# Reading the first two blocks' rows ahead of the second block's weights, in a two-layer cross-attention and experts kernel

## The chip, the cores and the metric

The kernel runs on one core of one Trainium2 chip. The metric is device time of one execution in microseconds (us): the median of three timed runs. Lower is better. One further execution was recorded by the hardware profiler. All rows below come from that one.

## The reference

The input is 8 x 512 tokens of width 256. Two layers follow each other. Each adds gated cross-attention and a gated feed-forward part. Only the last part matters here, the second layer's feed-forward, a mixture of 8 experts with the best 2 for each token:

```python
logits = x @ gate_w + gate_b                       # x: layernormed tokens, [4096, 256]
probs = softmax(logits); top_w, top_idx = top_k(probs, 2)
top_w = top_w / sum(top_w)
h = silu(x @ w1[e]) * (x @ w3[e])                  # for each expert e; w1, w3: 256 x 1024
out_e = h @ w2[e]                                  # w2: 1024 x 256
x = x + tanh(g_ffn[1]) * sum over the token's two experts of top_w * out_e
```

## The kernel before

The kernel is three stages, each in a program block of its own: `first_layer`, `cross_attention` and `experts`. A program block ends only when all engines have reached its end, and the engines then start the next one together.

Cross-attention also does the routing. For each token it finds two experts, and GpSimd (POOL) writes the token's row (256 values, its weight and its number) with an indirect DMA to two places of a table in HBM, `xs` (`expert_in` in the trace), one region for each expert. This is the scatter; each of its DMAs adds 16 to `routing.scattered` when it lands.

`experts` has two program blocks. The first, "route", does what remains once the last tokens are routed:

- POOL issues the last 8 scatter DMAs (L766) and waits for `routing.scattered` to reach its full count (L1711).
- VectorE (DVE) works out on one partition which expert and which first row each of the NBLK = 39 blocks of 256 rows has (L1727 to L1748). The results are the tiles `first_row` and `expert`. It then signals `blocks_known`.
- SyncE (SP) issues the weights of block 0 and of block 1 (`load_weights`). Each is three DMAs of 1 MB into the three tiles `raw[0..2]` (`m_raw`). There is one set of raw tiles, so block 1's load of `raw[n]` waits on `lo_done[n]`, until block 0's copy has been split out of it.
- ScalarE (ACT) rounds each raw tile to `w_hi` (`high_part`, L1673) and DVE takes the remainder to `w_lo` (`low_part`, L1677), for block 0 only.
- SP ends this program block by waiting until block 1's three weight tiles have landed (L1702).

The second, "run", is the experts' part: 39 blocks with two sets of tiles (`p` = 0 and 1). TensorE (PE) transposes the block's rows (`turn`, L1845), ACT and DVE split them, PE multiplies by w1 and w3 in three passes (`hidden`, 96 matmuls), and by w2 (`project`, 48 matmuls, L1852). While block j is computed, ACT and DVE split the weights of block j + 1: ACT's `high_part(j + 1)` of the tile n stands in its order behind the silu of f = 1, 3 and 5 of block j. SP in this block loads rows (`load`, L1787 and L1789) and then weights for each block j > 1, in a written order. POOL gathers the rows of the output that a block adds to (`fetch`, L1812) and scatters them back (`store`, L1819).

The order at the start of "run" before the change: SP loads the rows of blocks 0 and 1, then goes on with block 2's rows and weights. PE's first instruction is `turn(0, 0, 0)`, which waits on `x_in[0]`, that is, on the rows of block 0. A load of rows needs two things: a register load of the first row's number from `first_row`, and that the scatter has landed.

Of the kernel before, what the change touches and what calls it, by code (L numbers as in the profile page):

```python
# [11 lines left out]
P = 128  # L12
BATCH, SEQ, D = 8, 512, 256
T = BATCH * SEQ
NT = T // P
# [5 lines left out]
NE, TOPK = 8, 2  # L21
BLK = 256
NBLK = T * TOPK // BLK + NE - 1
ROWS = NE * T + NE * BLK
BT = BLK // P
WIDE = D + 2
# [737 lines left out]
def scatter_rows(pool, routing, xs, k, j):  # L764

    pool.indirect_dma_start(out=xs, out_offset=bass.IndirectOffsetOnAxis(ap=routing.pos[:, k, j:j + 1], axis=0),  # L766
                            in_=routing.XN[:, j, :], in_offset=None).then_inc(routing.scattered, 16)
# [863 lines left out]
def experts(nc, M1, X, ident_f, routing, xs, out):  # L1631
# [10 lines left out]
    with ExitStack() as ctx:  # L1642
        sb = lambda n, s, d=F32: ctx.enter_context(nc.sbuf_tensor("m_" + n, s, d))
        sem = lambda n: ctx.enter_context(nc.semaphore("m_" + n))
        two = lambda n, s, d=F32: [sb(f"{n}{p}", s, d) for p in range(2)]
        pair = lambda n: [sem(n + "0"), sem(n + "1")]
        expert = sb("expert", [1, NBLK], I32)
        first_row = sb("first_row", [1, NBLK], I32)
# [7 lines left out]
        w_raw_in = [sem(f"w_raw_in{n}") for n in range(3)]  # L1656
        hi_done, lo_done = [sem(f"hi_done{n}") for n in range(3)], [sem(f"lo_done{n}") for n in range(3)]
        h_ps, y_ps = sem("h_ps"), sem("y_ps")

        def load_weights(sp, j):  # L1660

            e = sp.value_load(expert[0:1, j:j + 1] if isinstance(j, int) else expert[0:1, bass.ds(j, 1)],
                              min_val=0, max_val=NE - 1)
            for n, w in enumerate((w1, w3, w2)):
                if not (isinstance(j, int) and j == 0):
                    sp.wait_ge(lo_done[n], j)
                sp.dma_start(raw[n][:, :, :], w[e].rearrange("(c p) n -> p c n", p=P)).then_inc(w_raw_in[n], 16)

        def high_part(act, j, p, n):
            act.wait_ge(w_raw_in[n], 16 * (j + 1))  # L1670
            if not (isinstance(j, int) and j < 2):
                act.wait_ge(*((h_ps, FC * (j - 1)) if n < 2 else (y_ps, BT * (j - 1))))
            act.activation(w_hi[p][n][:, :, :], raw[n][:, :, :], ACT.Copy).then_inc(hi_done[n], 1)  # L1673
# [8 lines left out]
        with ExitStack() as route:  # L1682
            sb = lambda n, s, d=F32: route.enter_context(nc.sbuf_tensor("r_" + n, s, d))
            sem_ = lambda n: route.enter_context(nc.semaphore("r_" + n))
            starts_i, starts = sb("starts_i", [1, NBLK, NE], I32), sb("starts", [1, NBLK, NE])
            per_e = lambda n, d=F32: sb(n, [1, NE], d)
            total, total_i, padded_i, padded, ends = per_e("total"), per_e("total_i", I32), per_e("padded_i", I32), per_e("padded"), per_e("ends")
            off = [per_e("off0"), per_e("off1")]
            past, skipped = sb("past", [1, NBLK, NE]), sb("skipped", [1, NBLK, NE])
            per_b = lambda n: sb(n, [1, NBLK])  # L1690
            n_past, sum_past, at, number = per_b("n_past"), per_b("sum_past"), per_b("at"), per_b("number")
            iotas, chain, blocks_known = sem_("iotas"), sem_("chain"), sem_("blocks_known")
            block = route.enter_context(nc.Block())
            B = BATCH - 1

            @block.sync
            def _(sp):
                sp.wait_ge(blocks_known, 1)
                load_weights(sp, 0)
                load_weights(sp, 1)  # L1700
                for n in range(3):
                    sp.wait_ge(w_raw_in[n], 32)  # L1702

            @block.gpsimd
            def _(pool):
                pool.iota(starts_i[:, :, :], pattern=[[BLK, NBLK], [0, NE]], base=0, channel_multiplier=0).then_inc(iotas, 1)
                for k in range(TOPK):
                    pool.wait_ge(routing.labelled, TOPK * B + k + 1)
                    for j in range(TPB):
                        scatter_rows(pool, routing, xs, k, j)  # L1710
                pool.wait_ge(routing.scattered, 16 * NT * TOPK)  # L1711

            @block.scalar
            def _(act):
                for n in range(3):
                    high_part(act, 0, 0, n)

            @block.vector
            def _(dve):
                steps = Steps(dve, chain)  # L1720

                def do(ins):

                    steps.done(ins)
                    steps.wait()

                do(dve.tensor_tensor(total[:, :], routing.ends_at[0:1, :], routing.region[0:1, :], ALU.subtract))  # L1727
                do(dve.tensor_scalar_add(total_i[:, :], total[:, :], float(BLK - 1)))
                do(dve.tensor_scalar(padded_i[:, :], total_i[:, :], -BLK, None, ALU.bitwise_and))
                do(dve.tensor_copy(padded[:, :], padded_i[:, :]))  # L1730
                do(dve.memset(off[0][:, 0:1], 0.0))
                do(dve.tensor_copy(off[0][:, 1:NE], padded[:, 0:NE - 1]))
                c, s = 0, 1
                while s < NE:
                    do(dve.tensor_copy(off[1 - c][:, 0:s], off[c][:, 0:s]))
                    do(dve.tensor_tensor(off[1 - c][:, s:NE], off[c][:, s:NE], off[c][:, 0:NE - s], ALU.add))
                    c, s = 1 - c, 2 * s
                do(dve.tensor_tensor(ends[:, :], off[c][:, :], padded[:, :], ALU.add))
                dve.wait_ge(iotas, 1)
                do(dve.tensor_copy(starts[:, :, :], starts_i[:, :, :]))  # L1740
                do(dve.tensor_tensor(past[:, :, :], starts[:, :, :], ends[:, :].unsqueeze(1).broadcast_to([1, NBLK, NE]), ALU.is_ge))
                do(dve.tensor_reduce(n_past[:, :], past[:, :, :], AX.X, ALU.add))
                do(dve.tensor_tensor(skipped[:, :, :], past[:, :, :], padded[:, :].unsqueeze(1).broadcast_to([1, NBLK, NE]), ALU.mult))
                do(dve.tensor_reduce(sum_past[:, :], skipped[:, :, :], AX.X, ALU.add))
                do(dve.scalar_tensor_tensor(out=at[:, :], in0=n_past[:, :], scalar=float(T), in1=starts[:, :, 0], op0=ALU.mult, op1=ALU.add))
                do(dve.tensor_tensor(number[:, :], at[:, :], sum_past[:, :], ALU.subtract))
                do(dve.tensor_copy(first_row[:, :], number[:, :]))
                dve.tensor_scalar(expert[:, :], n_past[:, :], float(NE - 1), None, ALU.min).then_inc(blocks_known, 1)  # L1748
                relabel(dve, routing, B)
                for n in range(3):  # L1750
                    low_part(dve, 0, 0, n)

        with ExitStack() as run:
            sb = lambda n, s, d=F32: run.enter_context(nc.sbuf_tensor("e_" + n, s, d))
            sem_ = lambda n: run.enter_context(nc.semaphore("e_" + n))
            two = lambda n, s, d=F32: [sb(f"{n}{p}", s, d) for p in range(2)]
            pair = lambda n: [sem_(n + "0"), sem_(n + "1")]
            w_hi[1] = [sb(f"hi1_{n}", shapes[n], F32R) for n in range(3)]
            w_lo[1] = [sb(f"lo1_{n}", shapes[n], F32R) for n in range(3)]
            xb = two("x", [P, BT, WIDE])  # L1760
            label = two("label", [P, BT, 2])
            x_hi, x_lo = two("x_hi", [P, KC, BLK], F32R), two("x_lo", [P, KC, BLK], F32R)
            silu = [X[:, n, :] for n in range(2)]
# [4 lines left out]
            ps_h = [ps[:, 2 + n, :] for n in range(4)]  # L1768
            ps_y = [ps[:, 6 + n, 0:D] for n in range(2)]

            x_in, x_used = pair("x_in"), pair("x_used")
            x_hi_done, x_lo_done = sem_("x_hi_done"), sem_("x_lo_done")
            silu_done, gated_done, g_parts = sem_("silu_done"), sem_("gated_done"), sem_("g_parts")
            g_high, y_left, y_out = sem_("g_high"), sem_("y_left"), sem_("y_out")
            labelled, blanks, before_in = sem_("labelled"), sem_("blanks"), sem_("before_in")
# [5 lines left out]
            @block.sync  # L1781
            def _(sp):
                def load(j, i, p):
                    if not (isinstance(j, int) and j < 2):
                        sp.wait_ge(x_used[p], i)
                        sp.wait_ge(labelled, j - 1)
                    at = sp.value_load(first_row[0:1, j:j + 1] if isinstance(j, int) else first_row[0:1, bass.ds(j, 1)],  # L1787
                                       min_val=0, max_val=ROWS - BLK)
                    sp.dma_start(xb[p][:, :, :], xs[bass.ds(at, BLK), :].rearrange("(n p) d -> p n d", p=P)).then_inc(x_in[p], 16)  # L1789
                    if not (isinstance(j, int) and j < 2):  # L1790
                        load_weights(sp, j)

                load(0, 0, 0)
                load(1, 0, 1)
                with sp.Fori(1, LAST // 2) as i:
                    for p in range(2):
                        load(2 * i + p, i, p)
                load(LAST, LAST // 2, 0)
# [275 lines left out]
```

## Time and profile before

| | |
|---|---|
| median of 3 runs | 2155.09 us (2154.49 to 2155.93) |
| profiled execution | 2156.33 us |
| its span | 2154.6 us |
| mean granted TensorE clock | 0.944 |
| PE busy | 1913.3 us (89%) |
| DVE busy | 1601.9 us (74%) |
| ACT busy | 1069.0 us (50%) |
| POOL busy | 919.2 us (43%) |

The span runs from the first to the last recorded instruction. The profiled execution's own time is 1.73 us longer than its span. Busy shares are means over three stages with different limits, so what a change in one place is worth has to be read from that place: from the waits and the chain of work there. An engine named with a q (SPq) is that engine's sequencer, which also issues DMAs.

### The profile page before, as it was taken

Reading aid. Unit: us, or ns where it says so; the run is one execution under the profiler, and the core shown is the slowest. Engines: PE = TensorE matmul, PEld = TensorE weight load, DVE = VectorE, ACT = ScalarE, POOL = GpSimd, SP = SyncE. Lnnn points to the kernel's source line nnn. Section 1 sums busy time; section 2 is a strip of 40 time slices with the busy share of each in tenths; the row PEclk is TensorE's granted clock in tenths of the full one; section 3 lists DMA queues with packets and bytes.
Section 4 is the critical chain, followed back from the end, with each engine's and each line's share of the span. In section 5 each row is a group of like instructions: output and inputs, shape, how many; then the busy total and the mean of one; then the engine's idle time right before and its main releaser. Section 6 shows DMA issues by size and latency. Waiting matters only on the chain. (4 is left out here: it accounts for less than half of the span.)

```text
span 2154.6 us, 35704 instructions
## 1 busy us (share of the span) xinstructions
PE 1913.3 (89%) x11904; PEld 1347.0 (63%) x11968; DVE 1601.9 (74%) x3393; ACT 1069.0 (50%) x2062; POOL 919.2 (43%) x682
## 2 busy tenths in 40 slices
PE   5889898987669999999999999919999999999998
PEld 2566666665323343343434343419999999999998
DVE  7999999997546667767776778436777777777775
ACT  2233334433326655555555555415656555556663
POOL 6988888884533334343534331111222222222222
PEclk8899999998859999999999999958999999999999
DMA  5222222220243251515142441045766666666661
GB/s 169 109 89 87 109 86 89 87 94 1 61 100 87 63 123 45 128 45 123 65 110 93 89 121 33 21 146 171 227 225 214 219 225 219 219 228 227 224 209 59
DMA packets 140065, 271.45 MB, mean 126 GB/s; under 512 B 13915, under 2 KB 91823, under 8 KB 134066
## 3 DMA queue, kind: packets, MB, share of 16 engines
q1 hardware_dynamic: 128812, 244.55, 36.7%
q0 software_dynamic: 10624, 25.26, 3.2%
q8 instruction: 56, 0.92, 0.2%
q14 instruction: 55, 0.45, 0.1%
q10 hardware_dynamic: 518, 0.27, 0.0%
HBM read 201.96 MB, written 71.39 MB: 127 GB/s over the span
## 5 line engine op out<-in xcount | busy, mean ns | idle before, releaser
L1434 DVE CUSTOM_DVE_ANT_0 x_dump<-x_ps,x_bias_q 128x512 bf16<-128x512 f32 x512 | 353.2, 690 | 100.6 <-PE x_ps L1127 87.9
L1303 ACT ACTIVATE x_PT<-x_ps 128x512 f32<-128x512 f32 x512 | 292.2, 601 | 225.7 <-PE x_ps L1142 222.6
L1819 POOL DMA_INDIRECT out_dram<-e_y,e_label x78 | 78.9, 1011 | 369.4 <-DVE e_y L1971 357.5
L1915 ACT ACTIVATE X<-m_ps 128x256 f32<-128x256 f32 x312 | 119.1, 382 | 232.6 <-PE m_ps L1852 232.6
L1127 PE MATMUL x_ps<-x_KS,x_QS 96*128 96x512 bf16 x512 | 201.3, 395 | 23.3 <-DVE x_mx L1434 22.6
L1142 PE MATMUL x_ps<-x_QS,x_KS 98*128 98x512 bf16 x512 | 195.7, 382 | 6.7 <-issue 2.6
L1954 DVE TENSOR_TENSOR X<-X,m_ps 128x256 f32<-128x256 f32 x312 | 120.9, 418 | 103.5 <-ACT X L1915 98.9
L1852 PE MATMUL m_ps<-e_x_lo,m_hi 128*128 128x256 f32 x640 | 181.4, 283 | 1.5 <-DVE e_x_lo L1939 1.5
L1852 PE MATMUL m_ps<-e_x_hi,m_lo 128*128 128x256 f32 x640 | 181.3, 283 | 0.0
L1852 PE MATMUL m_ps<-e_x_hi,m_hi 128*128 128x256 f32 x640 | 181.1, 283 | 0.0
L1141 PE MATMUL x_ps<-x_bias_k,x_ident_b 128*128 128x512 bf16 x448 | 171.3, 382 | 1.1 <-issue 1.1
L1852 PE MATMUL m_ps<-e_x_hi,e_hi 128*128 128x256 f32 x608 | 171.1, 281 | 0.0
L1852 PE MATMUL m_ps<-e_x_hi,e_lo 128*128 128x256 f32 x608 | 171.1, 281 | 0.0
L1852 PE MATMUL m_ps<-e_x_lo,e_hi 128*128 128x256 f32 x608 | 171.1, 281 | 0.0
L1677 DVE TENSOR_TENSOR m_lo<-m_raw,m_hi 128x2048 fp32r<-128x2048 f32 x60 | 137.3, 2289 | 36.4 <-ACT m_hi L1673 36.4
L285 POOL TENSOR_TENSOR a_pool_pv<-a_e,a_v 128x2304 f32<-128x2304 f32 x32 | 162.2, 5070 | 0.0
L1812 POOL DMA_INDIRECT e_y<-out_dram,e_label x78 | 82.8, 1061 | 163.7 <-DMA out_dram<-e_y,e_label 136.7
L1677 DVE TENSOR_TENSOR e_lo<-m_raw,e_hi 128x2048 fp32r<-128x2048 f32 x57 | 130.4, 2287 | 26.2 <-ACT e_hi L1673 26.2
L1127 PEld LDWEIGHTS x_ps<-x_KS,x_QS 96*128 96x128 bf16 x512 | 49.9, 98 | 141.7 <-DVE x_mx L1434 110.3
L1673 ACT ACTIVATE m_hi<-m_raw 128x2048 fp32r<-128x2048 f32 x60 | 115.0, 1917 | 20.8 <-DMA m_raw<-in_L_ffn_w_dram 20.8
L1852 PEld LDWEIGHTS m_ps<-e_x_lo,m_hi 128*128 128x128 f32 x640 | 121.7, 190 | 1.9 <-issue 1.9
L1852 PEld LDWEIGHTS m_ps<-e_x_hi,m_lo 128*128 128x128 f32 x640 | 121.7, 190 | 0.0
(301 smaller groups left out, 5409.1 us busy)
## 6 DMA issues: line engine op xcount, KB each, us to landing
m_raw<-in_L_ffn_w_dram SPq DMA_DIRECT2D x117, 1024.0 KB, 5.3
expert_in<-a_blank SPq DMA_DIRECT2D x34, 1032.0 KB, 4.3
parts<-x_part SPq DMA_DIRECT2D x24, 512.0 KB, 3.7
e_x<-expert_in SPq DMA_DIRECT2D x39, 258.0 KB, 4.8
next_mask_k<-in_maskT_dram SPq DMA_DIRECT2D x32, 256.0 KB, 2.6
next_mask_q<-in_mask_dram SPq DMA_DIRECT2D x29, 256.0 KB, 2.8
x_KS<-parts SPq DMA_DIRECT2D x16, 384.0 KB, 11.4
x_QS<-parts SPq DMA_DIRECT2D x8, 576.0 KB, 6.6
```

The lines of the kernel that those rows point to most:

```text
L285: pool.tensor_tensor(heads(pool_pv[:, :], PV_POOL), probabilities(e_[t % 2][:, PV_OWN * H:], PV_POOL), values(v_sb[t % 3][:, :], PV_POOL), ...
L1127: pe.matmul(ps_max[m % 2], QS[b % 2][0:HROWS, h, q * P:(q + 1) * P], KS[b % 2][0:HROWS, h, :], start=True, stop=True).then_inc(s1_ps, 1)
L1141: pe.matmul(ps_st[e % 3], ident_b[:, :], bias_k[b % 2][:, kc, :], start=True, stop=False)
L1142: pe.matmul(ps_st[e % 3], KS[b % 2][:, h, kc * P:(kc + 1) * P], QS[b % 2][0:HROWS + MROWS, h, :], start=False, stop=True).then_inc(st_read ...
L1303: act.activation(PT[unit % 2][:, k, :], ps_st[e % 3], ACT.Exp, scale=DH ** -0.5).then_inc(exp_done, 1)
L1434: dve.tensor_tensor_reduce(out=dump[:, :], in0=ps_max[m % 2], in1=bias_q[b % 2][:, q, :], scale=1.0, scalar=NEG, op0=ALU.add, op1=ALU.max, ...
L1673: act.activation(w_hi[p][n][:, :, :], raw[n][:, :, :], ACT.Copy).then_inc(hi_done[n], 1)
L1677: eng.tensor_tensor(w_lo[p][n][:, :, :], raw[n][:, :, :], w_hi[p][n][:, :, :].bitcast(F32), ALU.subtract)\
L1812: pool.indirect_dma_start(out=yb[p][:, n, :], out_offset=None, in_=rows, in_offset=tokens(p, n), bounds_check=T - 1, oob_is_err=False).the ...
L1852: mm = pe.matmul(out, left[a], right[b], start=first and n == 0, stop=last and n == 2)
L1915: act.activation(silu[f % 2], ps_h[f % 4][:, 0:BLK], ACT.Silu).then_inc(silu_done, 1)
L1954: dve.tensor_tensor(gated[k % 2][:, n, :], silu[n], ps_h[f % 4][:, BLK:2 * BLK], ALU.mult)\
```

## The change

In "route", SP no longer loads block 1's weights and no longer waits for them. It issues block 0's weights, waits until the whole scatter has landed, and then issues the rows of blocks 0 and 1. The row tiles `xb` and their semaphores `x_in` are allocated earlier so that this is possible. In "run", SP begins with block 1's weights. It then goes on with the loads of block 2 as before. The loads of blocks 2 to 38 keep their waits and their order.

```diff
+        xb = two("x", [P, BT, WIDE])
+        x_in = pair("x_in")
+
+        def load_rows(sp, j, p):
+            at = sp.value_load(first_row[0:1, j:j + 1] if isinstance(j, int) else first_row[0:1, bass.ds(j, 1)],
+                               min_val=0, max_val=ROWS - BLK)
+            sp.dma_start(xb[p][:, :, :], xs[bass.ds(at, BLK), :].rearrange("(n p) d -> p n d", p=P)).then_inc(x_in[p], 16)
...
                 sp.wait_ge(blocks_known, 1)
                 load_weights(sp, 0)
-                load_weights(sp, 1)
-                for n in range(3):
-                    sp.wait_ge(w_raw_in[n], 32)
+                sp.wait_ge(routing.scattered, 16 * NT * TOPK)
+                for j in range(2):
+                    load_rows(sp, j, j)
...
                 def load(j, i, p):
-                    if not (isinstance(j, int) and j < 2):
-                        sp.wait_ge(x_used[p], i)
-                        sp.wait_ge(labelled, j - 1)
-                    at = sp.value_load(...)
-                    sp.dma_start(xb[p][:, :, :], ...).then_inc(x_in[p], 16)
-                    if not (isinstance(j, int) and j < 2):
-                        load_weights(sp, j)
-
-                load(0, 0, 0)
-                load(1, 0, 1)
+                    sp.wait_ge(x_used[p], i)
+                    sp.wait_ge(labelled, j - 1)
+                    load_rows(sp, j, p)
+                    load_weights(sp, j)
+
+                load_weights(sp, 1)
                 with sp.Fori(1, LAST // 2) as i:
```

## Rows read from the trace of the kernel before

**Rows 1.** Chain of work that ended last, 1380 to 1462: start us, us, what.
```profile
1453.66 0.27 SPq L1787
...
1454.41 2.80 DMA e_x<-expert_in
...
1457.25 1.13 PE m_ps L1845 x4
```

**Rows 2.** The same chain, whole span, its longest pieces.
```profile
1459.87 14.14 PE m_ps L1852 x96
1474.45 17.14 PE m_ps L1852 x144
...
2122.87 22.79 PE m_ps L1852 x192
```

**Rows 3.** Waits of the SP queue, 1427 to 1454: us in total, times, longest.
```profile
SPq L1702 <- DMA m_raw<-in_L_ffn_w_dram: 7.7, 1, 7.7
```

**Rows 4.** Timeline of SP: start us, us, engine line op, count.
```profile
1427.55 1.45 SPq L1667 DMA_DIRECT2D m_raw<-in_L_ffn_w_dram  x3
...
1437.15 0.39 SPq L1667 DMA_DIRECT2D m_raw<-in_L_ffn_w_dram  x1
...
1445.15 0.37 SPq L1667 DMA_DIRECT2D m_raw<-in_L_ffn_w_dram  x1
...
1454.41 1.54 SPq L1789 DMA_DIRECT2D e_x<-expert_in  x2
```

**Rows 5.** Line L1667, 1427 to 1430, then 1437 to 1446: issue to landing.
```profile
DMA to landing us min/median/max: 5.2/9.2/12.3
...
DMA to landing us min/median/max: 6.2/6.7/8.0
```

**Rows 6.** Timeline 1415 to 1460, all engines; brackets hold idle before, and releaser.
```profile
1419.84 0.16 DVE L1620 COPY ends_at<-x_prior 128x8 f32<-128x8 f32 x1
...
1420.31 0.15 DVE L1727 TENSOR_TENSOR r_total<-ends_at,region 1x8 f32<-1x8 f32 x1 [0.30 <-PEq L780]
...
1432.16 0.96 POOL L766 DMA_INDIRECT expert_in<-XN,pos  x1 [0.30 <-issue]
...
1437.29 1.91 ACT L1673 ACTIVATE m_hi<-m_raw 128x2048 fp32r<-128x2048 f32 x1 [2.64 <-DMA m_raw<-in_L_ffn_w_dram]
1439.23 2.29 DVE L1677 TENSOR_TENSOR m_lo<-m_raw,m_hi 128x2048 fp32r<-128x2048 f32 x1 [2.26 <-ACT m_hi L1673]
1440.89 1.91 ACT L1673 ACTIVATE m_hi<-m_raw 128x2048 fp32r<-128x2048 f32 x1 [1.70 <-DMA m_raw<-in_L_ffn_w_dram]
...
1442.84 2.29 DVE L1677 TENSOR_TENSOR m_lo<-m_raw,m_hi 128x2048 fp32r<-128x2048 f32 x1 [1.31 <-ACT m_hi L1673]
1453.67 0.99 POOL L1823 MEMSET e_y<- 128x512 f32 x2 [20.55 <-POOLq L1682]
```

**Rows 7.** DMA queues, 1437.5 to 1438, then 1450 to 1453: packets, MB, share.
```profile
q0 software_dynamic: 2, 0.00, 0.2%
...
q1 hardware_dynamic: 74, 0.07, 7.0%
```

**Rows 8.** Timelines of ACT and DVE in block 0 of "run".
```profile
1465.65 1.91 ACT L1673 ACTIVATE e_hi<-m_raw 128x2048 fp32r<-128x2048 f32 x1
...
1468.63 1.91 ACT L1673 ACTIVATE e_hi<-m_raw 128x2048 fp32r<-128x2048 f32 x1
...
1471.48 1.93 ACT L1673 ACTIVATE e_hi<-m_raw 128x2048 fp32r<-128x2048 f32 x1
...
1475.44 1.48 DVE L1964 TENSOR_TENSOR e_g_lo<-X,e_g_hi 128x512 fp32r<-128x512 f32 x2
```

**Rows 9.** Windows: us; busy PE, PEld, DVE, ACT, POOL; PEclk, DMA share, GB/s.
```profile
1465.00:1466.00 1.00, 1.00 (x8) 1.00 (x8) 0.21 (x1) 0.63 (x2) 0.00 (x0) 0.74 0.00 0
...
556.00:558.00 2.00, 2.00 (x4) 0.35 (x2) 0.19 (x1) 0.00 (x0) 2.00 (x13) 0.61 1.00 292
```

**Rows 10.** Timeline of PE, start of the cross-attention stage.
```profile
554.67 3.39 PE L1093 MATMUL x_ps<-next_wkv,next_cT 128*128 128x512 f32 x4 [2.46 <-POOL x_half L977]
```

**Rows 11.** The page, DMA queues, whole span: packets, MB, share of 16 engines.
```profile
q8 instruction: 56, 0.92, 0.2%
```

More of the change, by code:

```diff
@@ L1759, in experts @@
             w_lo[1] = [sb(f"lo1_{n}", shapes[n], F32R) for n in range(3)]
-            xb = two("x", [P, BT, WIDE])
             label = two("label", [P, BT, 2])
@@ L1769, in experts @@
             ps_y = [ps[:, 6 + n, 0:D] for n in range(2)]
-            x_in, x_used = pair("x_in"), pair("x_used")
+            x_used = pair("x_used")
             x_hi_done, x_lo_done = sem_("x_hi_done"), sem_("x_lo_done")
@@ L1783, in load @@
                 def load(j, i, p):
-                    if not (isinstance(j, int) and j < 2):
-                        sp.wait_ge(x_used[p], i)
-                        sp.wait_ge(labelled, j - 1)
-                    at = sp.value_load(first_row[0:1, j:j + 1] if isinstance(j, int) else first_row[0:1, bass.ds(j, 1)],
-                                       min_val=0, max_val=ROWS - BLK)
-                    sp.dma_start(xb[p][:, :, :], xs[bass.ds(at, BLK), :].rearrange("(n p) d -> p n d", p=P)).then_inc(x_in[p], 16)
-                    if not (isinstance(j, int) and j < 2):
-                        load_weights(sp, j)
-                load(0, 0, 0)
-                load(1, 0, 1)
+                    sp.wait_ge(x_used[p], i)
[3 more added lines that the diff above has]
+                load_weights(sp, 1)
                 with sp.Fori(1, LAST // 2) as i:
```

## The prediction, made before the changed kernel was run

> **What bounds the kernel now.** I read the slices of the page first: PE is busy nine tenths or more in almost every slice of the experts' part, and one slice in the middle falls to one tenth. The views that matter are the ones of that hole. The chain of waits, from its end backwards, shows what the time after the hole is: one unbroken run of PE matmuls, 144 to a block, each next piece beginning where the last one ends, up to the last block [rows 2]. So whatever moves PE's first matmul of the experts' part moves the end by the same amount, unless a new gap opens later.
>
> Ahead of that run the chain holds SP's register load, the DMA of block 0's rows (2.80 us), and the four transposes at 1457.25 [rows 1]. SP starts this only at 1453.66, because every engine starts "run" together. What is late then? The waits of the SP queue name it: 7.7 us at L1702, on block 1's weights [rows 3]. The last of them was issued at 1445.15 [rows 4] and took 8.0 us to land [rows 5], so it landed at 1453.15. The other engines were done before: POOL had issued its last scatter by 1433.12 and then stood idle until 1453.67, and DVE's last split of block 0's weights ended at 1442.84 + 2.29 = 1445.13 [rows 6]. PE needs none of block 1's weights to start. It waits for a barrier that waits for them, and then for rows whose table has long been complete.
>
> **The change, part by part.**
>
> *Wait at L1702 removed.* The end of "route" becomes the latest of the other arrivals. DVE's is 1445.13.
>
> *Does SP arrive later than DVE?* It now waits for the scatter. The last packets of the scatter's queue (q0) are in the half microsecond to 1438 [rows 7]. The semaphore comes after the last packet, by an amount that no row gives alone; I allow 0 to 1 us, so 1438 to 1439. A register load and the issue behind it took 1454.41 - 1453.66 = 0.75 us, and the second rows' DMA ended its issue 1.54 us after the first began [rows 1, 4]. SP therefore issues block 0's rows at 1438.8 to 1439.8 and is through at 1440.3 to 1441.3, at least 3.8 us before DVE. Cost nothing, covered by DVE's and ACT's splits; without that cover it would be up to 2 us.
>
> *Do the rows land in time?* They lie behind block 0's third weight tile, which lands at 1440.9 (ACT takes it at 1440.89 [rows 6]). Their own time is 2.8 us [rows 1]. So block 0's rows land between 1442.6 and 1443.7, ahead of 1445.13. The row DMA's 2.8 us leaves the path.
>
> *Does block 0's third weight tile land earlier?* Block 1's first tile was issued at 1437.15 [rows 4], while it was still under way; now 0.5 MB of rows follow later instead of that 1 MB. From below the gain is nothing. From above it is what DVE allows: its second split ends at 1439.23 + 2.29 = 1441.52, so the third cannot start before 1441.5 instead of 1442.84, 1.3 us. The tail of block 1's last load speaks for nothing: from 1450 to 1453 the engines were 7.0% busy [rows 7], about one of 16, so a single engine finished alone at its own pace, with nobody to compete with. I take 0.
>
> *Barrier and PE's start.* From DVE's end to its next instruction across the previous barrier: 1419.84 + 0.16 to 1420.31, 0.31 us. Across this one: 1453.15 to 1453.66, 0.5 us [rows 1, 6]. I take 0.45 us, so PE's transposes start at 1445.6 instead of 1457.25.
>
> **Sum: 1457.25 - 1445.6 = 11.65 us less.** What follows the transposes (ACT, its table load, DVE, first matmul at 1459.87) keeps its lengths.
>
> *Block 1's weights moved into "run".* Three DMAs and one register load stand ahead of block 2's on SP. All three `lo_done` waits are already met. Their issue begins about 0.75 us after the barrier, at 1446.35, the others about 0.5 us apart each (three in 1.45 us [rows 4]). When they land I take from block 0's own load, also three at once with indirect traffic beside it: 5.2, 9.2 and 12.3 us after issue [rows 5], hence 1451.6, 1456.1 and 1459.7. When they are needed: ACT took them at 1465.65, 1468.63 and 1471.48 [rows 8], 8.40, 11.38 and 14.23 us after the transposes began, hence now 1454.0, 1457.0 and 1459.8. Each is just in time, the third by 0.1 us. There is more cover behind that: `project` starts at 1474.45, its third quarter (12 matmuls of 17.14/144 = 0.119 us each, 1.43 us a quarter) at 1477.3, and the third remainder it needs ended at about 1475.44 + 0.7 = 1476.1 [rows 2, 8]. So ACT may be 1.2 us late before PE waits. Cost 0; if that cover is gone, each microsecond of lateness beyond it is one microsecond of time.
>
> The page "DMA: Bandwidth & Descriptors" of the Trainium skill (section "Anatomy of one DMA") fits a DMA of the GpSimd path by about 2.0 us plus its bytes over 436 GB/s. For 3 x 1.05 MB issued together that would be 9.2 us, against 13.3 us from first issue to last landing in block 0's load here; by it the third tile would come at about 1455.6, over 4 us early, and the case of late weights below would fall away. The trace doesn't agree, and I go by the trace.
>
> *What is queued behind them on SP:* block 2's rows. Their wait on `labelled` is met at about 1448, after the weights' issue at 1447.8; nothing is held up. They lie behind 3 MB in the queue, landing by about 1461, and PE turns block 2 only after 1474.45 + 17.14 = 1491.6 [rows 2], less 11.65, 1480. Block 2's weights wait for DVE's splits as before. POOL's first `fetch` waits on DVE's label, not on SP, and its sum is wanted after `project`, over 20 us later. The steady state then has the same instructions, waits and bytes as before.
>
> *The clock.* In the profile the granted clock rose from half (1.2 GHz) to full (2.4 GHz) inside 1465 to 1466, mean 0.74 [rows 9], so at about 1465.5, some 5.6 us after the first matmul. At the start of cross-attention it rose inside 556 to 558 (mean 0.61, so about 1.56 us in), 2.9 us after PE began at 554.67 [rows 9, 10]. Half speed costs half its time. A rise 2.7 us sooner or later gives or takes 1.3 us. I take the same 5.6 us and keep 1.3 for the range.
>
> The profiled execution would take 2156.33 - 11.65 = 2144.7 us, and the median, 1.24 us below it, 2155.09 - 11.65 = **2143.4 us**.
>
> **The rivals.**
>
> *A. The third tile lands early as well* (up to 1.3 us more). Against it the lone engine of [rows 7]; for it the traffic taken away at 1437. 2142.1 us, chance 0.05.
>
> *B. Block 1's weights come late and PE waits for ACT.* For it: the margins of 0.1 to 2.4 us above, a register load slower than 0.75 us, and POOL's first gather beside them. Against it: block 0's load had the scatter beside it, which is no less. Third tile 2.5 to 5 us later than counted: PE waits 1.2 to 3.7 us, 2144.6 to 2147.1, centre 2145.8 us. Chance 0.10.
>
> *C. The change doesn't do what it says:* SP's scatter wait or the rows take the place of the weights' landing at 1453. It decides from 1445.13 on; no time is saved only if the rows land 10 us later than counted. The last q0 packets before 1438 speak against it. The same page of the skill says that the semaphore follows the last byte's receipt, slowest where the target is HBM, and puts most of its 2 us there; the scatter writes HBM. By that the rows would be issued by 1440.8 and land near 1443.6, still in time. 2155.1 us, chance 0.02.
>
> *D. Slower: instruction loading.* The engines' instructions come by DMA as well (56 packets, 0.92 MB on one of the queues [rows 11]). Before, "run" began with the DMA engines idle after 1453; now its code is fetched while 3 MB of weights fill them. A fetch of a PE, ACT or DVE piece that waits behind them in each of the first blocks would stop PE. It decides from 11.65 us in total; by the longest landing in this stretch, 12.3 us for each of two fetches, 24.6 - 11.65 = 13 us slower, 2168 us. Against it: block 0's splits ran at full pace while 3 MB landed, and steady blocks carry 3 MB each without a break in PE. Chance 0.03.
>
> **How the numbers follow.** My forecast has 0.80, with its own range of 2142.0 to 2144.8 (clock 1.3 us either way, barrier 0.15 us, spread of the runs 0.7 us); A 0.05, B 0.10, C 0.02, D 0.03. The range reaches down to A with a sooner clock, 2141.5, and up to the greater part of B, 2146.5. A measurement of this kernel tells a change of about 0.2% (4.3 us) from none. Forecast, A and B all lie beyond that: faster 0.95, same 0.02, slower 0.03.
>
> **What would show it right or wrong.** After: no wait at L1702; PE's first transposes about 0.45 us behind DVE's third split in "route"; two row DMAs issued near 1439 and three weight DMAs from about 1446.3; ACT's three splits of block 1's weights 8.4, 11.4 and 14.2 us behind the transposes, released by ACT's own order and not by a DMA; an unbroken chain of L1852 from then on. The forecast is wrong if ACT's third split names the weights' DMA as releaser with over 1.2 us of idle time, if SP is the last at the barrier, or if gaps open in PE in blocks 1 or 2.

## The result, and the profile after

Timed side by side, 12 runs each, the changed kernel took 2140.84 us (median, 2132.74 to 2147.83) and the kernel before 2154.55 us (2148.17 to 2160.16). The ratio is 0.9939, 95% interval 0.9923 to 0.9955: 13 us less, between 10 and 17. The forecast was 11.65 us less (0.9946) and 2143.4 us, with a range down to 2141.5; the measured time lies 0.7 us below that range. About 0.5 of these 0.7 us lie in the kernel before, which was counted from 2155.09 us in the forecast and has 2154.55 here; 0.9939 of 2155.09 would be 2141.9, inside the range. The sign and the mechanism at the hole were as forecast. Two other things happened to which the forecast's sum gave nothing: the matmuls of the odd blocks run faster, and the clock rises sooner.

The chain of waits of the kernel after, from 1440 on (start us, us, what), and its last large piece; it answers to [rows 1, 2]:

```profile
1450.91 1.10 PE m_ps L1846 x4
...
1452.04 0.61 ACT e_x_hi L1903
...
1453.51 13.39 PE m_ps L1853 x96
1466.89 0.44 PE m_ps L1846 x4
1467.33 16.99 PE m_ps L1853 x144
...
2109.84 22.57 PE m_ps L1853 x192
```

SP's register load and the DMA of the rows are gone from the chain. It goes back from the transposes straight to the barrier. But the transposes start at 1450.91, not at 1445.6 (the next paragraphs say why); and the segments of PE behind them are shorter than those in [rows 2]: 13.39 us instead of 14.14, and 16.99 instead of 17.14.

The waits of the SP queue (us in total, times, longest) answer to [rows 3]:

```profile
SPq L1663 <- DMA expert_in<-XN,pos: 9.9, 1, 9.9
...
SPq L1689 <- PEq L1689: 3.7, 1, 3.7
```

SP waits 9.9 us for the scatter, issues the rows, and then still waits 3.7 us at the barrier. It isn't the last to arrive.

The timelines (start us, us, engine line op) answer to [rows 4, 6, 8]:

```profile
1426.06 0.15 DVE L1734 TENSOR_TENSOR r_total<-ends_at,region 1x8 f32<-1x8 f32 x1 [0.30 <-PEq L780]
...
1433.32 1.45 SPq L1674 DMA_DIRECT2D m_raw<-in_L_ffn_w_dram  x3
1445.42 1.53 SPq L1665 DMA_DIRECT2D m_x<-expert_in  x2
1451.59 1.40 SPq L1674 DMA_DIRECT2D m_raw<-in_L_ffn_w_dram  x3
...
1446.36 1.91 ACT L1680 ACTIVATE m_hi<-m_raw 128x2048 fp32r<-128x2048 f32 x1 [1.07 <-DMA m_raw<-in_L_ffn_w_dram]
1448.30 2.29 DVE L1684 TENSOR_TENSOR m_lo<-m_raw,m_hi 128x2048 fp32r<-128x2048 f32 x1 [0.69 <-ACT m_hi L1680]
...
1458.67 1.91 ACT L1680 ACTIVATE e_hi<-m_raw 128x2048 fp32r<-128x2048 f32 x1
...
1461.52 1.93 ACT L1680 ACTIVATE e_hi<-m_raw 128x2048 fp32r<-128x2048 f32 x1
...
1464.40 1.93 ACT L1680 ACTIVATE e_hi<-m_raw 128x2048 fp32r<-128x2048 f32 x1
```

The first of these rows is the one to read first. Route starts at 1426.06 in this execution and at 1420.31 in that of before [rows 6]. All stages ahead of it run the same instructions in both kernels. So times after it have to be counted from it. From there to the transposes are 1450.91 - 1426.06 = 24.85 us, against 1457.25 - 1420.31 = 36.94. ACT's three splits of block 1's weights carry no bracket: no DMA held them.

For the comparisons below the span is cut into four stretches: up to the start of route (DVE's first instruction there), the *hole* (from there to PE's transposes), block 0 (from the transposes to the first segment of 144 matmuls), and the blocks (from there to PE's last matmul). In the profile before they are 1420.31, 36.94, 17.20 and 671.21 us; after, 1426.06, 24.85, 16.42 and 665.08 us.

The costliest groups (out<-in, shapes, count | busy, mean ns of one | idle before) say where the 6.1 us in the blocks come from. Of the kernel after:

```profile
L1853 PE MATMUL m_ps<-e_x_hi,m_lo 128*128 128x256 f32 x640 | 180.8, 282 | 0.0
...
L1853 PE MATMUL m_ps<-e_x_hi,e_hi 128*128 128x256 f32 x608 | 169.7, 279 | 0.0
...
L1853 PE MATMUL m_ps<-e_lo,e_g_hi 128*128 128x256 f32 x304 | 85.6, 282 | 0.0
```

Of the kernel before:

```profile
L1852 PE MATMUL m_ps<-e_x_hi,m_lo 128*128 128x256 f32 x640 | 181.3, 283 | 0.0
...
L1852 PE MATMUL m_ps<-e_x_hi,e_hi 128*128 128x256 f32 x608 | 171.1, 281 | 0.0
...
L1852 PE MATMUL m_ps<-e_lo,e_g_hi 128*128 128x256 f32 x304 | 87.1, 286 | 0.0
```

The names with m_ are the weight tiles of even blocks, those with e_ of odd blocks. Only the matmuls that read e_hi and e_lo are clearly faster, by 1 to 2 ns in `hidden` and by 4 to 5 in `project`; the means of the others changed by at most 1 ns. Nothing in the new order of loads singles out odd blocks. But the change also allocates xb (2 x 2064 bytes per partition, with rounding 4160) ahead of these six tiles instead of behind them, so they moved by 4160 bytes per partition; no other tile that L1853 reads did.

### The profile page after: what moved, and what is told of

Same layout as the page of the kernel before. It is cut to its first block and busy times, and to the rows that moved or that the text cites. A ratio compares the mean times of both kernels' runs of the same rounds, so it can differ in the third digit from the quotient of the medians.

```text
span 2141.3 us, 35766 instructions
## 1 busy us (share of the span) xinstructions
PE 1915.6 (89%) x11968; PEld 1347.2 (63%) x11968; DVE 1601.4 (75%) x3393; ACT 1068.8 (50%) x2062; POOL 923.3 (43%) x682
## 5 line engine op out<-in xcount | busy, mean ns | idle before, releaser
L1141 PE MATMUL x_ps<-x_bias_k,x_ident_b 128*128 128x512 bf16 x512 | 197.9, 386 | 2.3 <-DMA x_QS<-x_rows 1.2
L1853 PE MATMUL m_ps<-e_x_lo,m_hi 128*128 128x256 f32 x640 | 181.1, 283 | 1.5 <-DVE e_x_lo L1940 1.5
L1853 PE MATMUL m_ps<-e_x_hi,m_hi 128*128 128x256 f32 x640 | 180.9, 283 | 0.0
L1853 PE MATMUL m_ps<-e_x_hi,m_lo 128*128 128x256 f32 x640 | 180.8, 282 | 0.0
L1853 PE MATMUL m_ps<-e_x_lo,e_hi 128*128 128x256 f32 x608 | 170.3, 280 | 0.0
L1853 PE MATMUL m_ps<-e_x_hi,e_hi 128*128 128x256 f32 x608 | 169.7, 279 | 0.0
L1853 PE MATMUL m_ps<-e_x_hi,e_lo 128*128 128x256 f32 x608 | 169.6, 279 | 0.0
L1853 PEld LDWEIGHTS m_ps<-e_x_lo,m_hi 128*128 128x128 f32 x640 | 121.3, 190 | 1.9 <-issue 1.9
L1853 PEld LDWEIGHTS m_ps<-e_x_hi,m_hi 128*128 128x128 f32 x640 | 121.3, 190 | 0.0
```

What stands on the lines that cost most here:

```text
L1141: pe.matmul(ps_st[e % 3], ident_b[:, :], bias_k[b % 2][:, kc, :], start=True, stop=False)
L1853: mm = pe.matmul(out, left[a], right[b], start=first and n == 0, stop=last and n == 2)
```

## The experiments

Ratios are to the kernel before, run on the same chip. A mean over the profiles is used where single ones differ. ctl_before, g2_pad4160 and g3_xb_last were executed once each, so they give stretches and no ratio.

**ctl_before.** The kernel before, unchanged.

> The kernel before, unchanged, profiled once more. It tells what differs between executions of one program. Theory N (the differences outside the hole are spread between executions): route begins some us earlier or later than 1420.3, as it did after the change (1426.1), and the matmul segments of the experts' part differ from 17.09 us. Theory P (the pace of the experts' matmuls belongs to the place of the weight tiles): 144 matmuls take 17.08 to 17.09 us in every steady segment again, whatever the start of route.

Measured: 2156.42 us in the profiled execution. Route starts at 1422.87, the hole is 34.61 us, block 0 17.13, the blocks 671.15. So the hole of one and the same program differs by 2.3 us between two executions, while the 671 us of the blocks repeat to 0.06. The pace of the matmuls belongs to the program. The length of the hole is spread by microseconds in the old order.

**e1_place.** Only the allocation of the change, in the order of before.

```diff
+        xb = two("x", [P, BT, WIDE])
+        x_in = pair("x_in")
 
         def load_weights(sp, j):
...
-            xb = two("x", [P, BT, WIDE])
...
-            x_in, x_used = pair("x_in"), pair("x_used")
+            x_used = pair("x_used")
```

> The kernel before with only the allocation of the change: xb and x_in are allocated before the block-1 weight tiles e_hi and e_lo, which so lie 4160 bytes further on. The order of all instructions is that of before. Theory P: the matmuls that read e_hi and e_lo go from 281 ns to 279 (hidden) and 276 (project), a pair of blocks takes 34.7 us instead of 35.05, and the time falls by 6 us (0.28%), the hole staying as it was. Theory O (the pace follows from the new order of loads): pace and time as before.

Measured: 0.9969 (0.9953 to 0.9985), about 6.7 us less. Hole 35.31 us, block 0 17.48, the blocks 665.16 us. Its chain shows the two segments that were 17.14 and 17.09 us in the kernel before; from then on 17.00 and 16.85 us take turns, as after the change:

```profile
1476.30 17.06 PE m_ps L1853 x144
...
1493.80 16.86 PE m_ps L1853 x144
```

Theory P holds. Where xb is allocated is worth about half of what the change brought by the times (6.7 of 13 us) and a third by the profiles (6.1 of 17).

**e2_order.** The change, with every tile at its old address.

```diff
+        sb_e = lambda n, s, d=F32: ctx.enter_context(nc.sbuf_tensor("e_" + n, s, d))
+        w_hi[1] = [sb_e(f"hi1_{n}", shapes[n], F32R) for n in range(3)]
+        w_lo[1] = [sb_e(f"lo1_{n}", shapes[n], F32R) for n in range(3)]
+        xb = [sb_e(f"x{p}", [P, BT, WIDE]) for p in range(2)]
-        xb = two("x", [P, BT, WIDE])
...
-            w_hi[1] = [sb(f"hi1_{n}", shapes[n], F32R) for n in range(3)]
-            w_lo[1] = [sb(f"lo1_{n}", shapes[n], F32R) for n in range(3)]
```

> The change with all tiles at the addresses they have in the kernel before (e_hi and e_lo allocated early, ahead of xb). Theory P: PE's transposes start about 12 us sooner after the start of route than before, the steady segments take 17.09 us, and the time falls by 12 to 13 us less what the clock does, that is to about 0.9942 of before; the last 6 us of the profile's difference are missing and so the start of route must account for the rest. Theory O: segments of 17.00 and 16.85 us and a time equal to that of the change, 0.994 or lower.

Measured: 0.9965 (0.9947 to 0.9984), about 7.5 us less, between 3.4 and 11.4. Hole 24.40 us, block 0 16.44, the blocks 671.14. The blocks are back at the old pace to 0.07 us. This is the change that the forecast spoke of, alone. My expectation of 0.9942 lies just outside the interval; the 10.9 us that its profile is below the mean of the old order (0.9949) lie inside.

```profile
1444.11 1.10 PE m_ps L1847 x4
...
1460.55 17.08 PE m_ps L1854 x144
...
1478.07 17.09 PE m_ps L1854 x144
```

**e3_pad64.** The kernel before with unused bytes around the odd blocks' weights.

```diff
+            sb("pad0", [P, 16])
             w_hi[1] = [sb(f"hi1_{n}", shapes[n], F32R) for n in range(3)]
             w_lo[1] = [sb(f"lo1_{n}", shapes[n], F32R) for n in range(3)]
+            sb("pad1", [P, 16])
```

> The kernel before with 64 unused bytes per partition allocated ahead of e_hi and e_lo and 64 behind them, so that these six tiles start at a multiple of 128 bytes instead of 64 beyond one; all others keep their place within 128 bytes. Theory P128 (what matters is the place within 128 bytes): the matmuls reading e_hi and e_lo take 279 and 276 ns as after the change, 6 us less in all (0.997). Theory PD (what matters is another thing of the place, such as the distance to other tiles): 281 ns and the time of before.

Measured: 1.0002 (0.9982 to 1.0021); the blocks 672.24 us. The matmuls of `hidden` with e_hi and e_lo took 281 to 282 ns, those of `project` 279 to 285, and those of `hidden` with m_hi and m_lo rose from 283 to 285. P128 falls: the place within 128 bytes doesn't decide alone. Route started at 1430.71 here, the hole was 33.36 us.

**f0_change.** The changed kernel once more.

> The changed kernel once more, for a second profile and more times. If the start of route is spread between executions (theory N), it lies anywhere from 1419 to 1431 us and is not later for the new order; the stretch from route's first DVE instruction to PE's transposes is 24.4 to 24.9 us again (33.4 to 36.9 in the four profiles with the old order), and the stretch from block 1's first matmul segment to PE's end 665.1 us. Rival L (the new order or allocation makes the stages ahead of route longer): route starts near 1426 again, and the time falls by less than the 17 us that the profiles show behind it.

Measured: 0.9913 (0.9893 to 0.9933), 2135.63 us. Route starts at 1422.29, the hole is 24.38 us, block 0 16.20, the blocks 665.08. Theory N holds. Over all profiles of the study route starts at 1419.8 to 1430.7 with the old order (six profiles, mean 1423.7) and at 1418.5 to 1426.1 with weights moved or unwaited for (seven, mean 1422.5).

**f1_rows_in_run.** The weights moved, the rows read at the head of run.

```diff
                 load_weights(sp, 0)
-                sp.wait_ge(routing.scattered, 16 * NT * TOPK)
-                for j in range(2):
-                    load_rows(sp, j, j)
...
+                for j in range(2):
+                    load_rows(sp, j, j)
                 load_weights(sp, 1)
                 with sp.Fori(1, LAST // 2) as i:
```

> The change, but the rows of blocks 0 and 1 are read at the head of run, ahead of block 1's weights, as the kernel before does; only the weights have moved. My theory (the rows are worth their own DMA and register load): PE's transposes start 3.3 us later than after the change, 28.0 us from the start of route, and the time is 3 us above the change's. Rival R (the early rows are worth nothing, since the barrier or the third weight tile ends last anyway): 24.6 us.

Measured: 0.9949 (0.9932 to 0.9966). Hole 28.03 us, 3.5 above the mean of the changed order (24.54); block 0 16.05. My theory holds; the early rows are worth 3.5 us.

**f2_no_wait.** As f1, but block 1's weights are issued in route again; only the wait is gone.

```diff
                 load_weights(sp, 0)
+                load_weights(sp, 1)
...
-                load_weights(sp, 1)
                 with sp.Fori(1, LAST // 2) as i:
```

> The change's allocation, but block 1's weights are issued in route as in the kernel before, and only the wait for their landing is left out; rows at the head of run. Theory Q (rows queued behind a 1 MB tile land when that tile has): SP issues the rows at about 26 us from the start of route, they land no sooner than the last weight tile, about 32 to 34 us, and PE starts at 32 to 34 us, so that nearly all that the change earns at this place is missing. Theory W (the wait alone was the cost, rows pass by the weights on the other 15 engines): 28.0 us, as with the rows read late but the weights moved.

Measured: 0.9963 (0.9945 to 0.9981). Hole 30.79 us, between the two theories. The rows' DMA here, the last weight tile's time to landing here (issued at 1447.0), and the rows' DMA in f1_rows_in_run:

```profile
1448.46 4.77 DMA m_x<-expert_in
```

```profile
DMA to landing us min/median/max: 5.5/5.5/5.5
```

```profile
1451.14 2.73 DMA m_x<-expert_in
```

Counted from the start of route, the rows are issued 0.7 us later, since the last weights' issue waits for DVE's third split, and they take 2.0 us longer. The last weight tile landed at 1452.5 and the rows at 1453.23, 0.8 us behind it. So theory Q has the mechanism right, and W falls. The hole is shorter than Q's 32 to 34 us because the tile landed sooner than Q supposed, 30.0 us after the start of route.

**f3_third_later.** The change, and block 0's third split at the head of run.

```diff
-                for n in range(3):
+                for n in range(2):
                     high_part(act, 0, 0, n)
...
-                for n in range(3):
+                for n in range(2):
                     low_part(dve, 0, 0, n)
...
                 x_high(0, 0, 0)
+                high_part(act, 0, 0, 2)
                 hidden(0, 0)
...
                 x_low(0, 0)
+                low_part(dve, 0, 0, 2)
                 gate(0, 0, 0)
```

> The change, and the split of block 0's third weight tile (ACT's high part, DVE's low part) moved from route to the head of run, behind x_high and x_low, since hidden(0) doesn't need it. If the third split is what ends route last (my step), route ends at DVE's second split, 3 us sooner, and PE starts when the rows land, about 22.3 us from the start of route: 2 to 2.5 us below the change. Rival: ACT's 1.9 us ahead of the table load delays the first silu, or block 1's third tile, whose load now waits longer, stops PE before project(1); then PE shows idle time in blocks 0 or 1 and the gain is lost.

Measured: 0.9930 (0.9912 to 0.9949). Hole 21.54 us, 3.0 less than 24.54; block 0 16.16, the blocks 665.09, so nothing is given back. The times (2137.94 us) can't tell it from f0_change. Its chain names the next thing that is late, the scatter and then the rows:

```profile
1430.20 6.32 DMA expert_in<-XN,pos
...
1437.29 2.74 DMA m_x<-expert_in
...
1440.07 1.13 PE m_ps L1846 x4
```

**g1_all_moved.** f3_third_later, and xb ahead of the raw tiles, so that the even blocks' weights lie 4160 bytes further on too. The raw tiles move with them.

```diff
+        xb = two("x", [P, BT, WIDE])
         raw = [sb(f"raw{n}", shapes[n]) for n in range(3)]
...
-        xb = two("x", [P, BT, WIDE])
```

> The version with the third split in run, and xb allocated ahead of the raw tiles, so that block 0's weight tiles m_hi and m_lo lie 4160 bytes further on as well; e_hi and e_lo stay where the change has put them. Theory D (a weight tile's distance to the g and x tiles decides, the same 4160 bytes for each set): the matmuls reading m_hi and m_lo go from 281 to 279 (hidden) and 276 ns (project) too, the stretch from block 1's first segment to PE's end from 665.1 to 659 us, and the time is 6 us below that version's, 0.990 of before. Theory E (only the place of e_hi and e_lo mattered): m matmuls 281 ns, 665.1 us, 0.993.

Measured: **0.9847 (0.9824 to 0.9870)**, 2122.45 us, the fastest version of the study, 33 us below the kernel before. Hole 21.85 us, block 0 16.55, the blocks 654.15. Both theories expected a smaller gain, down to 659 us (D) or 665.1 us (E) for the blocks: the matmuls of `hidden` with m_hi and m_lo took 278 ns, those of `project` stayed at 281. Its chain shows something more:

```profile
1494.85 16.35 PE m_ps L1853 x144
...
1511.64 16.35 PE m_ps L1853 x144
...
1528.42 16.96 PE m_ps L1853 x144
```

The first and the third of these are the same code of the loop on the same tiles, in its first and second pass (blocks 2 and 3, blocks 4 and 5).

**g2_pad4160 and g3_xb_last.** The kernel before, with the odd blocks' weights at the new address and x and g 4160 bytes further on as well (g2), and with all weights in place and x and g 4160 bytes lower (g3).

```diff
+            sb("pad", [P, 1040])
             w_hi[1] = [sb(f"hi1_{n}", shapes[n], F32R) for n in range(3)]
```

```diff
-            xb = two("x", [P, BT, WIDE])
             label = two("label", [P, BT, 2])
...
             yb = two("y", [P, BT, D])
+            xb = two("x", [P, BT, WIDE])
```

> The kernel before with 4160 unused bytes per partition ahead of e_hi and e_lo; they lie at the address that the change gives them, and the x and g tiles lie 4160 bytes further on too. Theory A (the absolute address of the weight tile decides): e matmuls 279 and 276 ns, m matmuls as before, 665.1 us from block 1's first segment to PE's end. Theory D (the distance to the x and g tiles): e matmuls 281 ns as before, and m matmuls, whose distance to x and g has grown by 4160 bytes, slower or otherwise changed.

> The kernel before with xb allocated last; all weight tiles keep their address, the x and g tiles lie 4160 bytes lower. Theory D: both sets now have the distance to x and g that e_hi and e_lo have after the change, and all matmuls take 279 (hidden) and 276 ns (project), 659 us from block 1's first segment to PE's end. Theory A: all 281 ns, 671.2 us.

Measured: g2 669.29 us for the blocks, `project` with e_hi 284 ns and with m_hi 279; g3 666.24 us, 281 to 282 ns in `project` with e_hi and with m_hi, 280 in `hidden` with e_hi and 281 with m_hi. Neither the absolute address (theory A) nor the distance (theory D) alone foretells these.

## Why the prediction was right and where it was wrong

**The step that failed** is the one at the end of the part on SP's queue: "The steady state then has the same instructions, waits and bytes as before", costed at nothing. It holds for the order of loads: e2_order has 671.14 us in the blocks. It doesn't hold for the change, because of a part that I didn't cost at all: the tile xb allocated earlier. That moved six weight tiles, and odd blocks' matmuls ran 1 to 5 ns faster each. The term was taken as 0 and measured 6.1 us. Shown by e1_place (6.7 us less in time, 6.05 in the blocks' stretch) and e2_order (the same order without it).

**The barrier and the rows.** As forecast. The last to arrive in route is DVE with its third split. PE starts 24.85 us after the start of route, forecast 1445.6 - 1420.31 = 25.3. The step on the third tile landing no earlier holds as well: DVE's third split ended 24.53, 24.08 and 24.06 us after the start of route in the three profiles of the new order, and 24.08 to 24.82 after it in the six of the old one. SP issued the rows 19.4 us after the start of route, forecast 18.5 to 19.5.

**The size of the hole before.** Here a term was mis-sized the other way. I took its 36.94 us from the one profile there was. The six profiles with the old order have 33.36 to 36.94, mean 34.64; three with the new order 24.38 to 24.85, mean 24.54. The hole shrank by 10.1 us, not by 11.65: block 1's last tile landed unusually late in that profile. It took 8.0 us there, and 5.2 and 5.4 us in g2_pad4160 and g3_xb_last; in all three the transposes begin 4.0 to 4.1 us behind its landing. The runs split the 10.1: 3.85 for the wait (to f2_no_wait), 2.8 for the weights out of the rows' way (to f1_rows_in_run), 3.5 for the rows read early. The first of these is the least certain, since the old order's hole is spread by 3.6 us and f2_no_wait has one profile.

**The clock.** I kept 1.3 us either way for it. Block 0's stretch is 16.20 to 16.44 us in three profiles of the new order and 16.84 to 17.48 in six of the old one, 0.8 us less. The matmuls of that stretch are the same. The interval between two of them falls from 0.21 to 0.12 us, as the granted clock goes from 1.2 to 2.4 GHz, 6.1 to 6.6 us after the transposes' start in the new order (after, e2_order, f0_change), and 7.6 to 8.7 us after it in the six profiles of the old one. PE had stood idle for 28 to 29 us before it in the first case and for 37 to 41 in the second. But the idle time alone doesn't order the rises: 5.7 us after 32 us idle in f1_rows_in_run, 7.0 after 26 in g1_all_moved. Why the clock rises sooner was not tried and stays open.

**Sum.** 10.1 + 0.8 + 6.1 = 17.0 us by the profiles, against 13 (10 to 17) and 19 (14 to 23) in the two sets of times. The forecast's 11.65 us was for order alone, where the profiles give 10.9 and the times 7.5 (3.4 to 11.4). So the hole was counted too large and the allocation was left out, and the two errors partly cancelled: that 11.65 us came within 2 us of the measured 13 is in part luck. The missing allocation term pushed the total out of the range at its lower end; e2_order, the same order without it, took 2146.67 us, just above the upper end of 2146.5. The range itself had a slip: rival A with the clock 1.3 us sooner is 2142.1 - 1.3 = 2140.8 us, not 2141.5.

**The rivals.** A is not shown: the third split's end moved by less than its spread. B did not happen, but the margin was as thin as forecast. In the kernel after, block 1's tiles are issued at 1451.6, 1452.1 and 1452.6. The first two land 5.0 and 9.0 us later. The profile's row has no landing for the third. The trace has 15 of its 16 landing signals by 1462.94 and the last at 1464.23, 11.7 us after its issue (forecast 12.3). ACT took the tile at 1464.40, with 0.2 us to spare, and behind that stands, by the forecast's own count, 1.2 us before PE waits. The traffic fits this, 322 GB/s up to 1463 and 33 behind it (us; busy PE, PEld, DVE, ACT, POOL; PEclk, DMA share, GB/s):

```profile
1462.00:1463.00 1.00, 1.00 (x11) 1.00 (x10) 1.00 (x2) 1.00 (x1) 0.00 (x0) 1.00 1.03 322
1463.00:1463.50 0.50, 0.50 (x6) 0.50 (x6) 0.50 (x3) 0.50 (x2) 0.00 (x0) 1.00 0.11 33
```

In f1_rows_in_run the row of the third tile is complete; it was issued at 1454.4, landed at 1466.9, and ACT took it at 1467.02:

```profile
DMA to landing us min/median/max: 12.5/12.5/12.5
```

From the first issue to the last landing it is 12.6 us in the kernel after and 13.5 in f1_rows_in_run. I had priced this from block 0's load, 13.3 us with the scatter beside it, and that was near. The fit in the Trainium skill (page "DMA: Bandwidth & Descriptors", section "Anatomy of one DMA") is for a DMA of the GpSimd path; by it the three tiles take 9.2 us, an estimate. The traces of both runs, whose tiles SP loads, don't agree with it. C and D did not happen: SP is at the barrier 3.7 us before it opens, and PE shows no idle time in the first blocks. Block 0's rows landed 2.7 us after their issue, at 1448.1, which is 2.8 us before the transposes. So the scatter could have ended that much later at no cost. With the third split gone from route, in f3_third_later, it is what PE waits for.

**What stays open.** By what rule the place of the tiles sets the pace. It is not the place within 128 bytes, the address alone or the distance to x and g alone. In g1_all_moved the same code on the same tiles runs at two paces, and one segment of f2_no_wait took 17.05 us where the others of its kind took 16.84 or 16.85, so something besides the tiles' place enters. One rival was not tried: that it matters what the other engines and the DMAs read and write at the same moment.

## What to carry to other kernels

Cost the allocation in a diff like any other edit: a tile that is allocated earlier moves all those behind it, and where one engine's stream is the bound, about 2 ns on each of 2736 matmuls came to 6 us here, more than half of what the hole gave. When two profiles are compared, cut them at events that both have and compare stretch by stretch; here 5.75 us of difference ahead of the change hid in the span. A transfer's landing time from one profile is a sample: take its spread as part of the range before it is made a term. And a row with the least, the median and the greatest of three landing times doesn't say which is whose, nor that all three are in it: ask for each transfer by itself.

## What the runs showed of the hardware that was not expected

The time of a matmul of one shape depends on where its operands lie: group means of 276 to 290 ns in `project`, 278 to 285 in `hidden`. The blocks' stretch of one layout repeats to 0.2 us in 665 or 671 between executions. Moving two small tiles gave 6 us and, for the other set of weights as well, 17 us in all in the blocks (671.2 to 654.15). And a transfer of 258 KB, issued in the same queue 1.5 us behind one of 1 MB, took 4.77 us instead of 2.73 and landed 0.8 us after it. Three transfers of 1 MB issued together took 12.6 us to the last landing without the scatter beside them, and 13.5 in another run, against 13.3 us with it.
